# A fused attention and gated feed-forward kernel: PSUM mix copied by ScalarE and scaled by GpSimd, transposes placed among the 512-column score passes

## What is computed

```
q, k, v = einsum('bsx,xMnd->Mbnsd', x, qkv)
a    = einsum('bnsd,bntd->bnst', q, k) * 64 ** -0.5
bias = cumsum(rpe_bias)[:, s - t] where s >= t, else -30000
a    = softmax(a + bias)
x1   = layernorm(x + einsum('bnsd,ndx->bsx', a @ v, out_w))
xr, xk = mixes of x1 and of x1 shifted by one token (mu_r, mu_k)
out  = layernorm(x1 + sigmoid(xr @ W_r.T) * (square(relu(xk @ W_k.T)) @ W_v.T))
```

## Time and profile before

| | |
|---|---|
| runs | 1121.46 us median of 3 (1121.15 to 1122.28) |
| the profiled execution | 1119.69 us |
| its span, first to last instruction | 1118.0 us |
| PE busy | 1064.6 us, 95% of the span |
| DVE, ACT, POOL busy | 806.7, 731.7, 5.4 us |
| granted TensorE clock, mean | 0.989 of full |
| DMA | 162 GB/s mean |

### The profile page before, as it was taken

How to read it: one execution, slowest core, us unless ns; L and a number is a source line. 1 busy time by engine, 2 the same in 40 slices (tenths; PEclk the granted TensorE clock), 3 DMA queues, 4 the chain that set the end, 5 groups by cost and what they waited for, 6 DMA issues and landing times.

```text
span 1118.0 us, 21664 instructions
## 1 busy us (share of the span) xinstructions
PE 1064.6 (95%) x6975; PEld 754.0 (67%) x6975; DVE 806.7 (72%) x2129; ACT 731.7 (65%) x1870; POOL 5.4 (0%) x15
## 2 busy tenths in 40 slices
PE   5899999999999999999999999999999999999994
PEld 3666666765666776666776676777676677666774
DVE  2766566776667788777788777778877778877766
ACT  2666666765767676666676676777676767666643
POOL 1000000000000000000000000000000000000000
PEclk8899999999999999999999999999999999999997
DMA  7756767666666767567667666677756766765810
GB/s 174 163 159 161 181 167 173 156 157 159 160 158 170 182 152 182 156 156 186 170 161 180 164 156 166 161 176 176 183 152 162 168 172 156 186 157 151 242 55 21
DMA packets 116222, 180.72 MB, mean 162 GB/s; under 512 B 13680, under 2 KB 72960, under 8 KB 116112
## 3 DMA queue, kind: packets, MB, share of 16 engines
q1 hardware_dynamic: 112992, 176.85, 63.5%
q10 hardware_dynamic: 3120, 2.49, 0.9%
HBM read 58.41 MB, written 20.22 MB: 70 GB/s over the span
## 4 chain that ended last, share of the span: by engine, by line
PE 68%; DVE 5%; issue 5%; ACT 4%; DMA 2%; SPq 2%; DVEq 0%
PE ps_o L1081 20%; PE ps_rows L1040 18%; PE ps_t L1057 10%; PE ps_m L1015 7%; PE ps_m L1020 4%; PE ps_m L1097 4%; PE ps_o L1057 2%; ACT prob L542 2%; DVE pt L742 2%; DMA stacks<-k_lo 1%; SPq L314 1%; ACT pt L558 1%; DVE prob L720 1%; PE ps_rows L1136 1%; PE ps_t L1062 1%
## 5 line engine op out<-in xcount | busy, mean ns | idle before, releaser
L542 ACT ACTIVATE prob<-prob,low 128x128 f32<-128x128 f32 (+7 forms) x512 | 395.6, 774 | 109.5 <-DVE low L720 104.3
L720 DVE CUSTOM_DVE_ANT_0 prob<-ps_rows,table 128x128 f32<-128x128 f32 (+7 forms) x512 | 379.8, 750 | 44.6 <-PE ps_rows L1040 28.2
L1040 PE MATMUL ps_rows<-stacks 128*128 128x512 f32 (+3 forms) x1536 | 395.6, 369 | 10.0 <-issue 6.5
L1057 PE MATMUL ps_t<-ident_r,prob_r 128*128 128x128 f32 x1984 | 283.8, 262 | 11.3 <-ACT pt L558 4.6
L1057 PEld LDWEIGHTS ps_t<-ident_r,prob_r 128*128 128x128 f32 x1984 | 211.9, 141 | 95.7 <-issue 72.8
L1081 PE MATMUL ps_o<-pt,v_pair 128*64 128x512 f32 (+3 forms) x1536 | 268.9, 492 | 0.0
L1040 PEld LDWEIGHTS ps_rows<-stacks 128*128 128x128 f32 x1536 | 246.0, 190 | 31.5 <-issue 6.6
L742 DVE COPY pt<-ps_t 128x256 f32<-128x256 f32 (+2 forms) x320 | 178.1, 565 | 115.2 <-PE ps_t L1057 114.9
L1081 PEld LDWEIGHTS ps_o<-pt,v_pair 128*64 128x64 f32 x1536 | 101.6, 136 | 175.8 <-issue 163.5
L558 ACT ACTIVATE pt<-ps_t 128x512 f32<-128x512 f32 (+3 forms) x352 | 163.1, 463 | 81.6 <-PE ps_t L1057 81.1
L1015 PE MATMUL ps_m<-x_cur,w_cur 128*128 128x512 f32 x250 | 131.2, 606 | 4.2 <-ACT x_t L511 2.2
(11 more groups left out here) (127 smaller groups left out, 605.3 us busy)
## 6 DMA issues: line engine op xcount, KB each, us to landing
stacks<-k_hi SPq DMA_DIRECT2D x124, 256.0 KB, 4.5
stacks<-k_lo SPq DMA_DIRECT2D x124, 256.0 KB, 5.0
inv_all<-inverse_sums SPq DMA_DIRECT2D x128, 128.0 KB, 3.4
stacks<-q_hi SPq DMA_DIRECT2D x62, 256.0 KB, 4.0
stacks<-q_lo SPq DMA_DIRECT2D x62, 256.0 KB, 4.4
mix_transposed<-mix_sb SPq DMA_DIRECT2D x62, 256.0 KB, 3.6
table<-bias_by_distance SPq DMA_DIRECT2D x64, 192.0 KB, 3.8
mix_tile<-mix_transposed SPq DMA_DIRECT2D x24, 448.0 KB, 3.9
```

The lines of the kernel that those rows point to most:

```text
L542: nc.scalar.activation(row, row, ACT.Exp, bias=low[:, r:r + 1], scale=-1.0, accum_out=total[:, r:r + 1]).then_inc(s_exp, 1)
L720: nc.vector.tensor_tensor_reduce(prob[:, r % PSLOTS, 0:width], ps_rows[:, score_at(r):score_at(r) + width], table[n % 2][:, h, 0:width][:, ...
L1040: ins = nc.tensor.matmul(ps_rows[:, at + c0:at + c1], q_st(h, n)[:, P * i:P * i + P], k_st(h, n, low_part)[:, c0:c1], start=(low_part == 0 ...
L1057: ins = nc.tensor.transpose(t_bank[TBANK[k]][:, P * b:P * b + P].bitcast(F32R), prob_r[:, r % PSLOTS, at:at + P], ident_r[:, :])
```

## The change

1. **The mix.** ACT copies `ps_o` to `mix_sb` unscaled (`copy_mix`) and GpSimd multiplies it in place by `inv_all` (`scale_mix`). The bank `ps_o` is free after the copy (semaphore `mix_copied`), and SP stores after the scaling (`mix_scaled`). ACT's copies stand at the head of slot 6 (far half) and at the end of slot 11 (near half).
2. **The key's square** is on GpSimd (`square_key`), into a semaphore of its own that the value product waits for.
3. **Copies.** Bank 5 and the first half's inverse sums go from DVE to ACT.
4. **Banks.** `TBANK` changes: the third bank is now also used for k = 9 and 12 (slots 8 and 10), between the far half's copy and the near mix, and for 18 and 21 after that.
5. **Order on TensorE.** In slots 3, 6, 7, 10, 11 and 15 up to two transposes of the slot's row follow each 512-column score pass. So in slot 11 all eight come ahead of the near mix.
6. The transposes of the inverse sums and of `x1` are in F32R. DVE's slot V_PROJ (11) does the tile's work after the row work.

```diff
-EVACUATOR = "010110010100011001110111"
-TBANK = [k % 2 for k in range(16)] + [2, 0, 1, 2, 0, 1, 2, 1]
+EVACUATOR = "010111010100011001110111"
+TBANK = [0, 1] * 4 + [0, 2, 1, 0, 2, 1, 0, 1] + [0, 1, 2, 0, 1, 2, 0, 1]
+BEHIND_MIX = (9, 18)
+AMONG = (3, 6, 7, 10, 11, 15)
...
# GpSimd
+            def scale_mix(n, g):
+                pool.wait_ge(s_raw, 2 * n + g + 2)
+                pool.wait_ge(s_inv_all[g], 32 * n + 32)
+                nc.gpsimd.tensor_tensor(mix_sb[g][:, :], mix_sb[g][:, :], inv_all[g][:, :], ALU.mult).then_inc(s_o, 1)
+            def square_key(e):
+                pool.wait_ge(s_sig, e + 1)
+                nc.gpsimd.tensor_tensor(k_act[:, :], k_act[:, :], k_act[:, :], ALU.mult).then_inc(s_square, 1)
+            def step(n, prev, tile_too, more):
+                if prev:
+                    scale_mix(n - 1, 1)
+                if tile_too:
+                    square_key(n - TILE_LAG)
+                scale_mix(n, 0)
...
# ACT
-                if k == INV_BANK[1]:
+                if k in INV_BANK:
...
+            def copy_mix(n, g):
+                act.wait_ge(s_pv, 2 * n + g + 3)
+                act.wait_ge(s_mix_d[g], 16 * n + 16)
+                nc.scalar.activation(mix_sb[g][:, :], ps_o[:, :], ACT.Copy).then_inc(s_raw, 1)
...
+                    if prev and slot == MIX_FAR[1] + 1:
+                        copy_mix(n - 1, 1)
...
+                    if slot == MIX_NEAR:
+                        copy_mix(n, 0)
...
# DVE
-            def store_mix(n, g):
-                dve.wait_ge(s_pv, 2 * n + g + 3)
-                dve.wait_ge(s_mix_d[g], 16 * n + 16)
-                dve.wait_ge(s_inv_all[g], 32 * n + 32)
-                nc.vector.tensor_tensor(mix_sb[g][:, :], ps_o[:, :], inv_all[g][:, :], ALU.mult).then_inc(s_o, 1)
...
-                    nc.vector.tensor_tensor(k_act[:, :], k_act[:, :], k_act[:, :], ALU.mult)
...
# PE: transpose() now does one block
+                if block == b0:
+                    if k in BEHIND_MIX:
+                        pe.wait_ge(s_raw, 2 * n + 1 + BEHIND_MIX.index(k))
                     else:
                         engine, count = emptied(n, k)
                         pe.wait_ge(s_ev[engine], count)
...
-                    pe.wait_ge(s_o, 2 * n + g + 1)
+                    pe.wait_ge(s_raw, 2 * n + g + 1)
...
-                    for row in rows_ahead(n, more, slot):
-                        score(*row)
+                    blocks = ROWS[slot][1] + 1
+                    moved = 0
+                    for m, row in rows_ahead(n, more, slot):
+                        for which in range(len(passes(row))):
+                            score(m, row, which)
+                            c0, c1, _ = passes(row)[which]
+                            share = min(2, blocks - moved) if slot in AMONG and c1 - c0 == BANK else 0
+                            for block in range(moved, moved + share):
+                                transpose(n, slot, block, tile_too)
+                            moved += share
...
-                    transpose(n, slot, tile_too)
+                    for block in range(moved, blocks):
+                        transpose(n, slot, block, tile_too)
```

More of the change, by code:

```diff
@@ L124, in build @@
         prob = sb("prob", [P, PSLOTS, SEQ])
+        with nc.sbuf_tensor("inv_r", [P, NROWS], F32R) as inv_r:
+            pass
+        inv = sb("inv", [P, NROWS])
+        with nc.sbuf_tensor("x1_r", [P, C], F32R) as x1_r:
+            pass
+        x1 = sb("x1", [P, C])
         ident = sb("ident", [P, P])
@@ L685, in _ @@
             dve.sem_inc(s_o, 1)
+            dve.sem_inc(s_raw, 1)
             dve.sem_inc(s_chain, CH)
@@ L825, in step @@
                         bias(*row)
[L826 to L830, removed]
                     if slot in INV_READY:
@@ L1022, in project @@
                 ins.then_inc(s_proj, 1)
-            def score(n, r):
-                h, i = ROWS[r]
[L1027 to L1037, removed]
-                    c1 = max(c1, c0 + SHORTEST)
-                    for low_part in range(2):
-                        ins = nc.tensor.matmul(ps_rows[:, at + c0:at + c1], q_st(h, n)[:, P * i:P * i + P],
-                                               k_st(h, n, low_part)[:, c0:c1], start=(low_part == 0),
-                                               stop=(low_part == 1))
-                ins.then_inc(s_score, 1)
@@ L1045, in transpose, with passes @@
-            def transpose(n, r, tile_too):
-                pe.wait_ge(s_exp, NROWS * n + r + 1)
-                for k in (k for k in range(NBANKS) if BANKS[k][0] == r):
-                    _, b0, nb = BANKS[k]
-                    if TBANK[k] == 2 and 2 not in TBANK[:k]:
-                        pe.wait_ge(s_o, 2 * n + 2)
+            def passes(r):
+                at, width = score_at(r), P * (ROWS[r][1] + 1)
+                cut = min(BANK - at % BANK, width)
+                return [(c0, max(c1, c0 + SHORTEST), low_part) for c0, c1 in ((0, cut), (cut, width)) if c0 < c1
+                        for low_part in range(2)]
@@ new lines, in score @@
+            def score(n, r, which):
+                h, i = ROWS[r]
+                if which == 0:
+                    if n == 0 and i == 0:
+                        pe.wait_ge(s_first[h], 96)
+                    elif i % GROUP == 0:
+                        pe.wait_ge(s_stack[h], 96 * n + 96)
+                    pe.wait_ge(s_biased, NROWS * n + r + 3 - rows_since(r))
+                c0, c1, low_part = passes(r)[which]
+                at = score_at(r)
+                ins = nc.tensor.matmul(ps_rows[:, at + c0:at + c1], q_st(h, n)[:, P * i:P * i + P],
+                                       k_st(h, n, low_part)[:, c0:c1], start=(low_part == 0), stop=(low_part == 1))
+                if which == len(passes(r)) - 1:
+                    ins.then_inc(s_score, 1)
@@ L1052, in transpose @@
+            def transpose(n, r, block, tile_too):
+                k = next(k for k in range(NBANKS) if BANKS[k][0] == r and BANKS[k][1] == block // 4 * 4)
+                _, b0, nb = BANKS[k]
+                bank = t_bank[TBANK[k]].bitcast(F32R)
+                if block == 0:
+                    pe.wait_ge(s_exp, NROWS * n + r + 1)
+                if block == b0:
+                    if k in BEHIND_MIX:
+                        pe.wait_ge(s_raw, 2 * n + 1 + BEHIND_MIX.index(k))
                     else:
@@ L1115, in _ @@
             for r in range(LEAD):
-                score(0, r)
+                for which in range(len(passes(r))):
+                    score(0, r, which)
             pe.wait_ge(s_in_w, 64)
```

43 lines of the change are left out of this document (23 added, 20 removed).

## The result

The changed kernel takes **1144.85 us** in the median of 4 runs (1143.02 to 1146.05), the kernel before 1121.78 in runs on the same chip. The ratio is 1.0203, 95% interval 1.0187 to 1.0219: 23 us slower, where 5 us faster was forecast. It lies 16 us above the wide range of 1104 to 1129.

The account below looks back on a forecast made before the run. TensorE, busy 95%, was taken to bound the kernel. A gain of 0.2 us per step over 23 steps (4.6 us) plus 0.7 at the end made 5.3 us: 1116 us in the median, range 1110 to 1120, wide range 1104 to 1129.

Parts of the forecast that it names:

- What the moves cost on TensorE: Transposes moved among score passes: ten extra islands cost 0.2 us per step, 6 us in 31 steps.
- 0.02 per island: TensorE's cost in us for each extra island of transposes between score passes; low end 0, high end 0.07.
- +0.02 and +0.04: Slots 3 and 15: cost in us per step of their extra islands on TensorE, one and two.
- What the copies cost: Copies move from DVE to ACT, multiplies of 1.04 us and the square to GpSimd; GpSimd costs nothing unless a slower rival holds.
- the rival: GpSimd's two multiplies hold DVE for half their length: 0.4 us per step, 12 us, 1133 us; chance 13%.
- Slots 5 to 10: Row 10's scores 0.35 us later, yet row 14's start 0.1 earlier, with one new wait ahead of slot 10.
- Slots 10 to 15: Islands cost the 0.1 us gained, slot 13's 0.37 goes, the inverse is late next; TensorE gains 0.25, slot 15 returns 0.04.
- Slot 13's wait: TensorE's 0.37 us wait for DVE's copy goes, since row 11's transposes are done before the near mix.
- Multiplies: GpSimd's two multiplies of the mix, put at 1.04 us each.
- The end of the program: Last scaled mix off DVE's queue, less a possible 0.5 us output projection wait: 0.7 us of gain together.
- The limit near by: Second head's key DMAs, started by `k_lo`, land about 1 us ahead of their scores; TensorE can gain about that per step.
- The gain expected from lighter engines: TensorE's waits in slots 8, 10 and 13: 0.8 us per step, 25 us in 31 steps, at most.

Follow-up runs that it names:

- experiment 7: Changed kernel with transposes among score passes in slot 11 alone and GpSimd's near multiply held until the layernorm sums are done; 1115.13 us, ratio 0.9930.
- experiment 1: Changed kernel with the transposes of slots 3 and 15 back behind their projections; 1125.93 us, ratio 1.0049.
- experiment 8: Changed kernel with islands of one transpose instead of two in slots 3 and 15, number of islands unchanged; 1139.35 us, ratio 1.0141.
- experiment 6: Changed kernel with slots 3 and 15's transposes back behind the projections and GpSimd's near multiply held until the layernorm sums are done; 1119.36 us, ratio 0.9971.
- 10: Changed kernel with transposes among score passes in slot 11 alone, near multiply not held back; 1122.91 us, ratio 1.0002.
- experiments 3: Changed kernel with GpSimd's near multiply held back until the layernorm sums are done on DVE; 1140.18 us, ratio 1.0162.
- experiment 9: Kernel before plus a spare GpSimd multiply released by row 0's bias, to meet the second layernorm's add on DVE; 1137.33 us, ratio 1.0141.

## Why the prediction was wrong

Its account of the old kernel held, and so did most of its terms. Two costs were left out of the sum, and both are in places that it had named.

- **What the moves cost on TensorE: the step that failed first.** The prediction priced a moved transpose by where it goes to (an island between score passes) and not by what it leaves. Its 0.02 per island is small, though not what failed: the rows of the table from slot 5 to 7 and from 10 to 12 show 0.22 for six, 0.04 each at most, since changed banks and waits are in them too, and slot 11's three alone take 0.10 in experiment 7. The distances of the earlier trace rows are there again (the 512 pass behind two transposes 0.30, the two 0.13). But in slots 3 and 15 the transposes were the cover for the emptying of `ps_m`. The sum gave these two slots +0.02 and +0.04; by experiment 1 they cost 0.62 per step, and 18.9 us. That it is the cover is shown by TensorE's starts right behind the emptying (592.90 to 592.95, 604.01 to 604.07) together with experiment 8.
- **What the copies cost: the step that failed second.** GpSimd was put at nothing unless it held DVE, at 13%. It did hold DVE, though not as the rival had it: the rival had the first multiply hold row 11's bias and both halve DVE. No instruction with an input in PSUM was held, and beside the far multiply DVE's work kept its length. One add with both inputs in SBUF was, until the multiply's end. The rival's price of 17 us above the forecast compares with 6 to 8 us measured (experiments 6 and 7 against 1 and 10). The prediction's evidence against it, had a DVE instruction with one input and could not tell, as it said itself; a search for two-input instructions near the end of the near mix would have found the add.

  The trace also fits a rule that the prediction had not used: the Trainium skill ("SBUF — State Buffer", Summary: rules for kernel authors) says that of a DVE instruction with two SBUF inputs and a GpSimd instruction that reads SBUF the second to issue "fully blocks" until the first finishes. The add's end 0.15 us after the multiply's, at different overlaps in two kernels, agrees. No run here has the add issued first.
- **Slots 5 to 10: right.** Row 14's scores were to come 0.1 earlier with a new wait for row 12's bias. Freed of what slots 3 and 15 add, they come 0.11 earlier (experiment 1), and the wait is there (`low`, 7.2 us in 23). That is no luck: the chain runs as told, with row 10's bias 0.32 later (0.35 by the sum), `k_lo` 0.08 behind an idle DVE (0.15) and row 12's bias 0.11 earlier (0.1).
- **Slots 10 to 15: half right.** The inverse was the next to be late, as said, and without the hold it comes 0.15 earlier than before (experiment 6), where 0.25 was counted. Slot 13's wait did not go. A transpose still waits for the copy at 621.75, which stands behind row 0's bias; of its 0.37 us 0.17 went. The copy that is waited for is that of row 12's first bank, before the change too (578.03 in the step of the earlier trace rows). It stood behind a copy of row 11 and row 0's bias. The prediction took away the first and forgot the second.
- **Multiplies** take 1.28, not 1.04:

```profile
L500 POOL TENSOR_TENSOR mix_sb<-mix_sb,inv_all 128x512 f32<-128x512 f32 x64 | 81.9, 1280 | 951.1 <-ACT mix_sb L614 951.1
```

  Since the add waits for the multiply's end, those 0.24 us are an estimated 5 of the 6 to 8 us (22 steps).
- **The end of the program**, counted at 0.7 of gain, gave none: from the last step's first scores to the end it is 72.2 us before and 72.3 after.
- **The limit near by** was real: the `k_lo` DMAs took part of the gain in experiments 3 and 7.

With both costs undone the kernel takes 1119.4 (experiment 6), 3.2 under the one before it; the sum said 5.3. So the forecast comes near for a kernel that this change is not.

The gain expected from lighter engines was there too, but the islands of slots 6, 7 and 10 gave part of it back, above all by delaying row 10's scores; slot 11 alone keeps 4.2 us more (experiment 7 against 6).

## What to carry to other kernels

A work item that is moved has two prices: what it costs where it goes, and what it covered where it stood. Before moving it, look for a single-buffered tile (here the projection's bank) whose release ran under it. Work put on an idle engine is free only if it doesn't hold a busy one: look on DVE for instructions with both inputs in SBUF near each GpSimd instruction, and release the GpSimd one behind them.

## What the runs showed of the hardware

- A DVE add of 128x128 with two SBUF inputs takes 0.28 us alone. Beside a GpSimd multiply of 1.28 that started first it takes 0.53 to 0.72 (changed kernel, 19 steps) or 0.84 to 1.06 (experiment 9, 22 steps), and in all 41 it ends 0.15 after the multiply. Copies from PSUM (0.69) and instructions with one input in PSUM and one in SBUF keep their lengths (biases, 0.28 to 1.22; the scaling of the mix, 0.69).
- A GpSimd multiply of two 128x512 SBUF tiles takes 1.28 to 1.30 us, whether DVE reads PSUM or SBUF beside it; the one of a tile by itself takes 1.04. Whether the second operand makes that difference was not measured.
- Parts of a change can be worth far more together than apart: the new order alone +115 us, the rest of the change without it +39, both +23, and both with the order cut to slot 11 and the multiply held back -7.
